# Attention in fp32 by two-part products: which of VectorE's two steps comes first in a slot

## The reference

```
ada = silu(c) @ W_ada + b_ada
shift_msa, scale_msa, gate_msa, shift_mlp, scale_mlp, gate_mlp = split(ada, 6)
h = layernorm(x) * (1 + scale_msa) + shift_msa
q, k, v = heads(h @ W_qkv + b_qkv)                    # 16 heads of 36
o = softmax(q @ k.T * 36 ** -0.5) @ v
x = x + gate_msa * (o @ W_proj + b_proj)
h = layernorm(x) * (1 + scale_mlp) + shift_mlp
x = x + gate_mlp * (gelu(h @ W_fc1 + b_fc1) @ W_fc2 + b_fc2)
U, _ = qr(P);  R = expm(skew(silu(cond) @ W.T + b))
out = x + ((x @ U) @ R - x @ U) @ U.T
```

## Time and profile before

| | us |
|---|---|
| Median of 3 runs | 2760.5 (2746.45 to 2760.8) |
| The profiled execution, its own time | 2755.61 |
| Its span | 2754.0 |
| TensorE matmul busy | 2410.4 (88%) |
| VectorE busy | 1435.6 (52%) |
| ScalarE busy | 1080.7 (39%) |
| GpSimd busy | 776.1 (28%) |

### The profile page before, as it was taken

How to read it: one execution, slowest core, us unless ns; L and a number is a source line. 1 busy time by engine, 2 the same in 40 slices (tenths; PEclk the granted TensorE clock), 3 DMA queues, 4 the chain that set the end, 5 groups by cost and what they waited for, 6 DMA issues and landing times. The chain is left out here.

```text
span 2754.0 us, 48999 instructions
## 1 busy us (share of the span) xinstructions
PE 2410.4 (88%) x15225; PEld 2040.4 (74%) x15225; DVE 1435.6 (52%) x2966; ACT 1080.7 (39%) x2298; POOL 776.1 (28%) x1548
## 2 busy tenths in 40 slices
PE   5698978879788897988976487999999999999998
PEld 1565757657576675666743286999999999999998
DVE  3577776777777777677761453333232323333332
ACT  1265555555555555555660212222222222222221
POOL 1043343333434344344451730111111111111110
PEclk9799989989999898999988657999999999999999
DMA  6122122221222222122113511010101010101100
GB/s 221 33 70 66 56 65 66 80 62 55 73 59 76 63 58 83 47 76 67 54 58 115 158 47 50 27 38 31 38 27 38 27 38 27 38 27 38 35 25 26
DMA packets 90983, 160.83 MB, mean 58 GB/s; under 512 B 23488, under 2 KB 34960, under 8 KB 90704
## 3 DMA queue, kind: packets, MB, share of 16 engines
q1 hardware_dynamic: 77840, 110.61, 13.9%
q0 software_dynamic: 11856, 46.60, 5.2%
q10 hardware_dynamic: 1024, 0.26, 0.0%
HBM read 80.23 MB, written 20.30 MB: 37 GB/s over the span
## 5 line engine op out<-in xcount | busy, mean ns | idle before, releaser
L1626 PE MATMUL bank<-h2T,w 128*128 128x256 f32 x4032 | 530.5, 283 | 8.8 <-issue 6.0
L1626 PEld LDWEIGHTS bank<-h2T,w 128*128 128x128 f32 x4032 | 507.5, 191 | 10.4 <-issue 7.2
L1537 DVE TENSOR_TENSOR glo<-bank,ghi 128x256 fp32r<-128x256 f32 x288 | 122.4, 425 | 719.8 <-ACT bank L1507 719.8
L1639 PE MATMUL bank<-w,ghi 128*128 128x288 f32 x2304 | 483.2, 301 | 7.0 <-DVE glo L1537 4.4
L1506 ACT ACTIVATE ghi<-bank,b 128x256 fp32r<-128x256 f32 x288 | 136.9, 475 | 734.6 <-PE bank L1626 734.6
L844 DVE TENSOR_TENSOR plo<-pf,phi 128x512 fp32r<-128x512 f32 x512 | 366.0, 715 | 85.7 <-ACT pf L720 81.1
L837 DVE TENSOR_REDUCE negm<-bank 128x1 f32<-128x512 f32 x512 | 349.2, 682 | 80.9 <-PE bank L983 66.7
L717 ACT ACTIVATE phi<-bank 128x512 fp32r<-128x512 f32 x512 | 302.9, 592 | 225.1 <-PE bank L1011 199.0
L1639 PEld LDWEIGHTS bank<-w,ghi 128*128 128x128 f32 x2304 | 369.1, 189 | 13.2 <-issue 7.6
L1639 PE MATMUL bank<-w,glo 128*128 128x288 f32 x1152 | 341.2, 296 | 0.0
L720 ACT ACTIVATE pf<-bank 128x512 f32<-128x512 f32 x512 | 303.2, 592 | 0.0
(11 more groups left out here) (213 smaller groups left out, 3283.6 us busy)
## 6 DMA issues: line engine op xcount, KB each, us to landing
xln<-x POOLq DMA_DIRECT2D x16, 1152.0 KB, 6.7
qs<-qkhi SPq DMA_DIRECT2D x192, 72.0 KB
ks<-qkhi SPq DMA_DIRECT2D x192, 72.0 KB
wst<-w_fc POOLq DMA_DIRECT2D x34, 288.0 KB, 3.1
x_d<-xln POOLq DMA_DIRECT2D x32, 288.0 KB, 2.5
xa<-x_d SPq DMA_DIRECT2D x32, 288.0 KB, 2.8
xs<-x_d SPq DMA_DIRECT2D x16, 576.0 KB, 3.8
out<-xs SPq DMA_DIRECT2D x16, 576.0 KB, 2.9
```

Of the source, the lines that this page charges most:

```text
L1626: mm = pe.matmul(F[ft % 2][:, 0:CH], w1[0:rows, w, ft * PAR:(ft + 1) * PAR], h[0:rows, a, :], start=(i == 0), stop=(i == len(FULL_PASSES) ...
L1639: mm = pe.matmul(Y[2 * tt + half][:, 0:HALF], g[ft % 2][:, span], w2[:, ft, w, half * HALF:(half + 1) * HALF], start=(ft == 0 and i == 0), ...
```

## The change

In VectorE's `slot`, the two first steps change places. The subtraction of slot n is issued first, the row maximum of slot n + 9 second. All else, on VectorE and on the other engines, stays as it is: the same instructions, the same waits, the same buffers.

```diff
                 def slot(b, n, phase):
+                    if is_there(b, n):
+                        p_los(b, n)
                     if is_there(b, n + MAX_LEAD - 1):
                         row_max(b, n + MAX_LEAD - 1)
-                    if is_there(b, n):
-                        p_los(b, n)
                     if n % TT == 2 and is_there(b, n - TT):
                         read_o(b, n)
```

## The result

| | before | after |
|---|---|---|
| Median, timed in turn on one chip (us) | 2759.6 (2746.45 to 2760.8) | 2783.2 (2781.0 to 2786.7) |
| Span of the profiled execution (us) | 2754.0 | 2782.4 |
| Its mean granted TensorE clock | 0.933 | 0.928 |
| TensorE matmul busy (us) | 2410.4 | 2418.2 |
| VectorE busy (us) | 1435.6 | 1432.6 |

The ratio is 1.0095, with an interval of 1.007 to 1.0119: the change makes the kernel 0.95% slower, 26 us (19 to 33). The forecast was 16 us slower, 2772, in a range of 2750 to 2787.

A forecast was written before the change was run, and what follows sets the result against it. TensorE idles 40.3 us for subtractions, but slot 40's later wait for GpSimd's elimination step takes the gain. 4.2 + 4.2 + 4.2 + 2.8 + 1.2 - 0.6 = 16.0 us on 2755.6 gave 2772, range 2750 to 2787.

The forecast's parts named there:

- line to slot 40: Slots 29 to 32: later output read delays GpSimd's load of x and the end of slot 40's wait; 4.2 us.
- units: Slots 21, 17, 2 and 61: splits behind the pair come later and TensorE waits; 4.2 us plus 4.2 us.
- last batch: Slots 49 and 57: rows copied for the elimination step come 0.6 us later; 1.2 us.
- first batch: Slots 18, 19 and 27: earlier subtractions give back 0.6 us, bounds 0 and 1.8.
- Part 1: Burst of statistics, slots 36 to 40: subtractions 0.60 us earlier, swallowed by slot 40's elimination-step wait; 0 us kept.
- Part 2: Slots 29 to 32: output read 0.60 us later, so slot 40's wait ends 0.60 later in 7 batches; 4.2 us.
- Part 3: Other work behind the pair moves back up to 0.60 us, in slots 21, 17, 2, 61, 43 to 49 and the last batch.
- slots 43 to 47: Late modulated x and slot 47's gain about cancel; the row copied in slot 48 leaves 0.4 a batch, 2.8 us.
- Rival 1: Subtractions come early and it pays: 53 waits each cut by up to 0.60, at most 32 us, 2724; chance 0.08.
- Rival 2: All is covered: slack meets part 3's delays and a shorter landing makes up part 2's; 2755 to 2760; chance 0.24.
- Rival 3: Slower still: 0.25 us waits in all 53 places, 2785, or lower clock behind slot 40, 2783; chance 0.16.
- deadline: Row maximum still ahead of the score product two slots later, except a 0.25 us wait where TensorE waits for the subtraction.

The follow-up runs named there:

- run 2: Kernel before, with the subtraction ahead of the row maximum in slots 28, 29 and 30 alone: 1.0019 (1.0003 to 1.0035), 5.2 us.
- run 3: Kernel before, with the subtraction first in slots 42 to 48 alone: 1.0028 (1.0015 to 1.004), 7.7 us.
- run 4: Kernel before, with the subtraction first in slots 1, 2, 16, 17, 20, 21, 60 and 61 alone: 1.0034 (1.0022 to 1.0047), 9.4 us.
- run 1: Kernel before, with the subtraction first in slots 36 to 41 alone, the burst of statistics: 1.0007 (0.9993 to 1.002).
- run 5: Changed kernel, with the row maximum first again in slots 1, 2, 16, 17, 20, 21, 28 to 30, 42 to 48, 60, 61: 1.0028, 7.7 us against kernel before.
- run 10: Kernel before, with the subtraction first in slot 47 alone: 0.9993 (0.9979 to 1.0008).
- run 11: Kernel before, with the subtraction first in slots 42 to 46 alone: 1.0015 (1.0 to 1.003), 4.1 us.
- run 7: Changed kernel, with GpSimd's elimination step of slot 39 ahead of the inverse deviation: 1.0000 (0.9983 to 1.0016) against the kernel before.
- Run 8: Kernel before, with the subtraction first and the row maximum behind the slot's reads and units, ahead of the statistics only: 1.0081 (1.0064 to 1.0097).
- run 6: Kernel before, old order, with GpSimd's elimination step of slot 39 ahead of the inverse deviation: 0.9945 (0.9928 to 0.9961), 2737.7 us.

## Why the prediction was right, and where it was too small

**Direction: right. Mechanism: right in the line to slot 40 and in the units, 12.6 of the 16.0 us; too small, and in part another one, in the rest.** Runs 2, 3 and 4 each cost time at the places named, run 1 gained nothing, and run 5, all the other slots, costs 7.7 us more. The sum of runs 2 to 5 is 5.2 + 7.7 + 9.4 + 7.7 = 30 us, each good to about 4 either way, against 26 (19 to 33) for the whole change. "Same" had been given a little more chance than "slower" (0.48 and 0.44), and by the prediction's own rule the two are 0.49 and 0.41, since 0.25 + 0.24 and 0.25 + 0.16 is what it adds up. The table has the terms of the sum with what answers to them. The rows overlap: runs 3 and 4 change slots of the first and of the last batch too, and the whole batch contains its share of the rows above.

| term | forecast, us | measured, us |
|---|---|---|
| burst, slots 36 to 40 | 0 | +1.9, from L250 to the broadcast (run 1: 1.7 by trace, 1.0007 by time) |
| line to slot 40 | 4.2 | 5.2 (run 2, 0.8 to 9.6) |
| slots 21, 17, 2, 61 | 8.4 | 9.4 (run 4, 6 to 13) |
| slots 43 to 49 | 2.8 | 7.7 (run 3, 4 to 11) |
| last batch | 1.2 | about 4 of its 6.75 (2.2 of them are in run 3 too) |
| first batch | -0.6 | +3.6 for the whole batch |

- **Part 1** held in what mattered: waits behind the burst swallow the early subtractions, shown by run 1. It named the wait in slot 40 alone and missed the one in slot 39, where the read of the output now stands 0.6 us further behind the subtraction. Its sentence that 726.90 "does not move by this" failed by a small amount, since it counted VectorE's instructions and not what they do to GpSimd's. L250 takes 0.53 instead of 0.23 us in all seven batches. From L250 to the broadcast, the seven batches sum to 40.2 us against 38.3.
- **Part 2** held to the hundredth at the read (0.60), and on average at the broadcast (0.58 in run 2). The wait in slot 40 was forecast to grow by 1.2 us. It grew by 0.28 in b = 3 (4.99 to 5.27), by 1.19 in b = 5 (4.74 to 5.93) and by 0.73 on average in the loops. The 1.2 counted the same thing twice: the burst itself starts 0.6 later, so its subtractions, 0.6 earlier within it, come when they did. From slot 28 TensorE reaches slot 39 after 26.81 us instead of 26.87, and the broadcast comes 0.89 later (33.46 to 34.35), the 0.6 of this part and the 0.3 of L250. The read was also placed wrongly, "1.2 us instead of 0.6 us after slot 30's subtraction ends": in the rows it starts 0.81 and now 1.41 us after that subtraction starts, 0.13 and 0.73 after it ends.
- **Part 3, slot 21**: 0.33 to 0.92 us, 0.36 to 0.96 on average. Right. **Slot 17**: 0.29 to 0.47, the 0.2 assumed. **Slot 2**: taken at 0.2 by slot 17's form; the wait there went from 0 to 0.64, past the upper bound of 0.6. In slot 17 the wait for ScalarE's high part covered 0.4 of the 0.6; in slot 2 TensorE waits for a split of v, as in slot 21, and nothing covered it; I took the wrong row as the nearest. **Slot 61**: 0.36 to 0.46.
- **Part 3, slots 43 to 47: the term that was too small.** It said that the late modulation and the gain of slot 47 "about cancel", 0.4 kept. From the broadcast of slot 40 to `values` of slot 48 the changed kernel takes 0.55 to 1.65 us longer, 1.1 on average in the loops. Three things were missed. The gain of slot 47 is there but does not last: run 10 loses it by slot 48, where TensorE waits for ScalarE instead (by 0.70 more in the changed kernel). The wait for hT in slot 43 grows by 0.72 (1.29 to 2.01). And behind it slots 44 and 45 run at the lower clock for longer, 0.76 us a batch without any wait; the prediction priced the clock only behind slot 40. Run 3 shows the size in the time (7.7) and run 11 that the late modulation is enough for most of it by the traces (0.89 of 1.10 us a batch). That the clock follows from the longer wait for hT is argued from the order of the rows: kernels with the old order there took 4.1 to 4.5 us for slots 44 and 45, run 7 took 4.65, run 11 4.68, run 3 4.91, the changed kernel 4.98.
- **Last batch**: priced 0.6 at each of two places. It grew by 6.75 us; against the first `values` of the batch 1.5 of this is there by slot 21, 1.3 more by slot 40 and 4 between slots 40 and 63, in steps of 0.8 at slot 41, 1.0 at slot 49 and 0.9 at slot 57, with 1.1 in small pieces between slots 50 and 56. TensorE's wait in slot 49, b = 7 (it answers to the earlier trace rows):

```profile
1438.27 0.66 PE L970 MATMUL bank<-chol,pick 128*128 128x64 f32 x2 [3.74 <-POOLq L613]
```

  It grew from 2.92 to 3.74, more than the 0.6 of the row's delay, and that broadcast already runs at the lower clock (0.66 us, against 0.41 before). From `values` of slot 48 to that of slot 60 TensorE was granted 0.85 of its clock, and now 0.74; it is busy for 18.8 us there instead of 17.3.
- **First batch**: no gain. Its subtractions come early as forecast, but in slots 11 and 19 TensorE then waits 0.59 us for the read of the output, where it had waited 0.55 and 0.56 for the subtraction; the waits of slots 18 and 23 went. By slot 40 the batch is 0.9 us longer, by slot 48 3.5, which is all of its growth. These eight slots were granted 0.88 of the clock and are granted 0.76.

**Rivals.** Rival 1, the early subtraction that pays, is refuted by run 1 and by the change itself: the waits for the subtraction fell by nearly half and the kernel got slower. The page of the Trainium skill that the prediction named ("Perfetto Trace Analysis", "Optimization Strategies") asks to optimize the engines "that are blocking the critical path", and rival 1 left out that condition; with it the trace does not speak against the page, since in the burst a later wait ends at its own time. Rival 2, all covered, is refuted by runs 2 to 4. Rival 3 had two halves. The new wait for row maxima came on the weight loads, up to 0.5 us ahead of the score product and up to 1.0 ahead of the transposed maxima. The prediction had 0.25 and said that it would be wrong if such waits appeared beyond 0.3; by that sign its deadline was too kind, though what reaches the matmuls is 0.08 us a time at the one and up to 0.6 at the other (7.8 us in 19 places, with the read of the output ending last). Run 8 shows what the wait is when the deadline is missed. Its clock half did not come as it was told: behind slot 40 the clock came back sooner, not later, and in run 1, where the wait in slot 40 grows by 0.7 us, slots 44 and 45 take 4.31 us against 4.22. It came behind the waits for hT, where no one had priced it, at 6.1 us in seven batches against the rival's 11. That, the waits for the read of the output (7.8) and the last batch are the largest parts that the sum of 16 did not have; no single new wait is large.

**What stays open**: the division of run 5's 7.7 us beyond the burst's 2, what slot 48 alone adds between runs 3 and 10 + 11, how far the longer wait for hT is the cause of the longer low stretch behind it, and the 5 us of the stages behind the attention. The traces are one execution of each kernel.

## What to carry to other kernels

A gain at the wait that shows most is worth nothing while a later wait, fed by another line, ends at its own time: look for what ends last before the next stage, and move that (here 15 us for one GpSimd step put ahead of another, against a loss of 26 us for helping the engine's most frequent wait). When two steps change places, the one that goes behind isn't the only thing that loses: everything queued behind the pair does, wherever the pair used to fill a gap. Follow each of these to the engine that consumes it and to that engine's queue too. And price what TensorE's clock does behind a wait that grows, since a good part of the term that was too small here was that: the same matmuls, without a wait, at the lower level for longer.

## What the runs showed of the hardware

A short instruction on GpSimd is held by some of what VectorE does beside it. L250, 128x4, took 0.23 or 0.24 us in all seven batches where VectorE was on a row maximum, and 0.53 or 0.54 in all seven where it was on a subtraction, in every kernel with the burst in the new order and its step in the old place (the changed one, runs 1, 5 and 8). The two are of equal length on VectorE (683 and 716 ns in the groups). It is not slowed down evenly. Wherever the subtraction had started first, L250 ended 0.09 or 0.10 us behind the subtraction's end, whether it then took 0.31 us (run 7), 0.37 (run 6) or 0.53. Where L250 had started first, by 0.06 to 0.10 us (four batches of run 6), it took 0.23 beside the same subtraction. So the order of two equal steps on one engine changed the time of a third on another, by what was left of the subtraction.
